# Graph attention beside experts: gathers issued at another pace, last softmax piece and lane carry ahead of the last expert unit

## The reference, cut to what matters

```python
# graph attention, 4 heads x 4 experts = 16 columns; 32768 random edges, and one self loop per node
h = (x @ W_gat).reshape(M, HEADS, NUM_EXPERTS)
e = leaky_relu(a_src[src] + a_dst[dst]); e_max = segment_max(e, dst); ee = exp(e - e_max[dst])
alpha = ee / (segment_sum(ee, dst)[dst] + 1e-16)
agg = segment_sum(h[src] * alpha[:, :, None], dst) + b_gat
scores = layernorm(agg).reshape(M, HEADS, NUM_EXPERTS).mean(1); top_k(scores, 2) -> softmax -> gates
# dense experts, all four on all rows
for ei in range(4):
    out += g_ei * (gelu(x @ W1[ei] + b1[ei], approximate=False) @ W2[ei] + b2[ei])
```

## Time and profile before

| | |
|---|---|
| median of 3 runs | 2281.04 us (2280.89 to 2281.67) |
| the profiled execution's own time | 2285.36 us |
| its span in the profile | 2283.6 us |
| busy: PE, DVE, POOL, ACT | 1666.2, 1276.7, 1076.5, 712.2 us |
| mean granted share of PE's clock | 0.851 |
| gathers of the stage (L1490), first and last start | 777.6 and 1153.7 us |
| up 19 on PE ends; the 37 steps end | 1131.3 us; 1236.0 us |

### The profile page before, as it was taken

How to read it: one execution, slowest core, us unless ns; L and a number is a source line. 1 busy time by engine, 2 the same in 40 slices (tenths; PEclk the granted TensorE clock), 3 DMA queues, 4 the chain that set the end, 5 groups by cost and what they waited for, 6 DMA issues and landing times. The chain is left out here.

```text
span 2283.6 us, 32653 instructions
## 1 busy us (share of the span) xinstructions
PE 1666.2 (73%) x8780; PEld 1319.3 (58%) x8781; DVE 1276.7 (56%) x3698; ACT 712.2 (31%) x1566; POOL 1076.5 (47%) x1102
## 2 busy tenths in 40 slices
PE   2776566766777799999934646565756799996997
PEld 1444344444445577777723546555645699984786
DVE  7877777667677410222146636555656566656235
ACT  1001146555651222222204632232323233312222
POOL 1676666555660566666640065555555554300000
PEclk9987578788789799999966867777777799997999
DMA  5233233333332122232251543433333565611001
GB/s 165 78 89 92 73 98 104 96 104 103 101 97 74 29 70 70 69 91 70 76 158 8 177 129 117 133 118 118 116 112 114 166 219 197 201 37 42 0 1 57
DMA packets 165026, 226.82 MB, mean 99 GB/s; under 512 B 35764, under 2 KB 124118, under 8 KB 162070
## 3 DMA queue, kind: packets, MB, share of 16 engines
q0 software_dynamic: 47392, 105.58, 16.5%
q1 hardware_dynamic: 114176, 115.99, 15.7%
q10 hardware_dynamic: 3318, 3.59, 0.5%
HBM read 172.48 MB, written 105.03 MB: 122 GB/s over the span
## 5 line engine op out<-in xcount | busy, mean ns | idle before, releaser
L473 POOL DMA_INDIRECT edge_rows<-xn_table,edge_source x391 | 376.5, 963 | 402.2 <-ACT held L2111 177.6
L2123 PE MATMUL part<-coef,held 128*128 128x128 f32 x2368 | 400.8, 317 | 215.7 <-issue 181.0
L473 POOL DMA_INDIRECT shared_space<-xn_table,edge_source x391 | 402.4, 1029 | 277.8 <-issue 108.5
L2123 PEld LDWEIGHTS part<-coef,held 128*128 128x128 f32 x2368 | 371.4, 228 | 254.6 <-issue 199.3
L2161 DVE SCALAR_TENSOR_TENSOR window_sums<-window_sums,fine_keep,part 128x256 f32 x592 | 282.4, 477 | 295.9 <-remote 130.2
L763 PE MATMUL part<-shared_space,hot 128*128 x832 | 297.9, 495 | 123.9 <-issue 63.4
L2111 ACT ACTIVATE held<-edge_rows 128x256 f32 x592 | 213.9, 408 | 484.6 <-PE part L2123 228.3
L1490 POOL DMA_INDIRECT gall<-attention_table,attention_source x256 | 244.9, 957 | 132.5 <-issue 68.3
L763 PEld LDWEIGHTS part<-shared_space,hot 128*128 128x128 f32 x832 | 176.7, 239 | 194.2 <-issue 173.4
L1148 DVE TENSOR_TENSOR shared_space<-shared_space,part 128x257 f32 x416 | 174.6, 420 | 132.8 <-remote 43.5
L2148 DVE SCALAR_TENSOR_TENSOR coef<-iota,fine_target,slot_coefs 128x128 f32<-128x128 f32 x592 | 203.7, 346 | 6.8 <-PEq L1283 6.8
(11 more groups left out here) (467 smaller groups left out, 1926.4 us busy)
## 6 DMA issues: line engine op xcount, KB each, us to landing
basis_sums<-window_sums SPq DMA_DIRECT2D x74, 1024.0 KB
z<-basis_sums SPq DMA_DIRECT2D x21, 1024.0 KB
expert_rows<-ys SPq DMA_DIRECT2D x20, 640.0 KB
shared_space<-expert_rows SPq DMA_DIRECT2D x25, 512.0 KB, 4.7
W<-in_L_ffn_W SPq DMA_DIRECT2D x20, 512.0 KB
gall<-attention_digits SPq DMA_DIRECT2D x32, 256.0 KB
xn_table<-shared_space SPq DMA_DIRECT2D x10, 640.0 KB, 4.1
shared_space<-xn_table,edge_source POOLq DMA_INDIRECT x391
```

Of the source, the lines that this page charges most:

```text
L473: pool.indirect_dma_start(rows[:, b % ring, 0:D], None, table, bass.IndirectOffsetOnAxis(ap=esrc[:, b:b + 1].bitcast(U32), axis=0)).then_i ...
L2123: mm = nc.tensor.matmul(part[n][:, c * P:(c + 1) * P], held[n][:, c * P:(c + 1) * P], coef[n][:, :, :].rearrange("p b w -> p (b w)"), star ...
```

## The change

Five things are edited together. (1) The gate ahead of group i of the gathers is at 9i/16 halves instead of 5i/8, so that a group is let go every 0.5625 halves instead of every 0.625, and the last at 35.4 halves instead of 39.4. (2) The pieces start behind units 6, 11, 15 and 17. (3) The last piece is no longer cut up between tiles: it runs as a whole behind unit 17, with its exponentials in the middle of ACT's unit 19, and the lane step ENDS follows at once. (4) On PE the four small blocks stand ahead of down 19 instead of behind it; on DVE the work along the lanes stands ahead of unit 19's tiles. For this the small blocks use PSUM banks 0 and 1 (of `up`), and the steps' banks move. (5) `ended` lies in the first weight buffer instead of in `hid`, so that POOL may gather the ends as soon as up 18 is through and the sums are stored; the blocks of the 37 steps move to the second weight buffer, and PE waits for the last tile's evacuation ahead of step 1.

```diff
-AFTER_UNIT = [8, 14, 18, 19]
+AFTER_UNIT = [6, 11, 15, 17]
 def experts_before(i):
-    half, part = divmod(5 * i, 8)
+    half, part = divmod(9 * i, 16)
...
-        return kind, done * per + per * part // 8
+        return kind, done * per + per * part // 16
...
+        ended = free[:, 0:NT * EW].rearrange("p (t w) -> p t w", w=EW)          # free is W1[0]
...
-        lines_ps = ps[0:GW, 7, :].rearrange("p (n q) -> p n q", n=4)
-        carry_ps = ps[:, 6, 0:EW]
+        lines_ps = ps[0:GW, 0, :].rearrange("p (n q) -> p n q", n=4)
+        carry_ps = ps[:, 1, 0:EW]
...
             pool.wait_ge(sums_out, 16 * PIECES)
+            pool.wait_ge(h_ready, (UNITS - 1) * 2 * FC)
...
-                for c in range(PIECES):
-                    if min(AFTER_UNIT[c] + 2, UNITS - 1) == m:
+                    if m == UNITS - 1 and n == FC - 1:
+                        exponents(PIECES - 1)
+                for c in range(PIECES - 1):
+                    if AFTER_UNIT[c] + 2 == m:
                         exponents(c)
...
-            down(UNITS - 1)
+            pe.wait_ge(h_used, UNITS * 2 * FC)
             pe.wait_ge(carry_steps, ENDS)
             nc.tensor.matmul(lines_ps[:, 0, :], sums[:, GT - 1, 0:GW], att.after[:, :], start=True, stop=True)
...
+            down(UNITS - 1)
             pe.wait_ge(carry_steps, RUN)
...
+            pe.wait_ge(y_used, UNITS * CT)
             turn_relations(0)
...
             for m in range(UNITS):
+                if m == UNITS - 1:
+                    carry_lanes()
...
                         parts = piece(c)
                         next(parts)
+                        if c == PIECES - 1:
+                            for _ in parts:
+                                pass
+                            lane_ends()
```

More of the change, by code:

```diff
@@ L1343, in attention_and_experts @@
         done = hid[0][:, :, :].rearrange("p f n -> p (f n)")
-        ended, crossed = (done[:, n * NT * EW:(n + 1) * NT * EW].rearrange("p (t w) -> p t w", w=EW) for n in range(2))
-        done = done[:, 2 * NT * EW:]
+        crossed = done[:, 0:NT * EW].rearrange("p (t w) -> p t w", w=EW)
+        done = done[:, NT * EW:]
         acc, sq = (done[:, n * NT * C16:(n + 1) * NT * C16].rearrange("p (t k) -> p t k", k=C16) for n in range(2))
@@ L1835, in piece, with lane_ends, carry_lanes @@
                 yield
+            by_head = lambda x: x[:, 0:C16].rearrange("p (h e) -> p h e", e=EXPERTS)
+            def lane_ends():
+                link.note(V.tensor_copy(by_head(last_top[:, :]), sums[:, GT - 1, GW:EW].unsqueeze(2).to_broadcast([P, H, EXPERTS])))
+                link(V.tensor_copy(last_top[:, C16:GW], sums[:, GT - 1, GW:EW]))
+                dve.sem_inc(carry_steps, 1)
+            def carry_lanes():
+                dve.wait_ge(carry_replies, LINES)
+                link.note(V.tensor_copy(first_of[:, :], lines_ps[:, 2, :]))
+                link(V.tensor_copy(chained[:, :], lines_ps[:, 3, :]))
+                link(V.tensor_tensor(chained[:, :], chained[:, :], first_of[:, :], ALU.mult))
+                link.note(V.tensor_scalar(chained[:, :], chained[:, :], BIG, -BIG, ALU.mult, ALU.add))
+                link(V.tensor_tensor(run[:, :], lines_ps[:, 1, :], first_of[:, :], ALU.mult))
+                link(V.tensor_scalar(first_of[:, :], first_of[:, :], BIG, -BIG, ALU.mult, ALU.add))
+                link(V.tensor_tensor(first_of[:, :], first_of[:, :], run[:, :], ALU.add))
+                link(V.tensor_tensor_scan(peak[:, 1:P + 1], chained[:, :], first_of[:, :], -BIG, ALU.add, ALU.max))
+                link.note(V.tensor_tensor(factor[:, 0, :], peak[:, 0:P], peak[:, 1:P + 1], ALU.subtract))
+                link(V.tensor_tensor(factor[:, 1, :], first_of[:, :], peak[:, 1:P + 1], ALU.subtract))
+                link(V.tensor_tensor(factor[:, 0, :], factor[:, 0, :], chained[:, :], ALU.add))
+                link(V.tensor_scalar(factor[:, :, :], factor[:, :, :], 0.0, None, ALU.min))
+                dve.sem_inc(carry_steps, 1)
+                dve.wait_ge(carry_replies, EXPONENTS)
+                link(V.tensor_tensor(first_of[:, :], factor[:, 1, :], lines_ps[:, 0, :], ALU.mult))
+                link(V.tensor_tensor_scan(run[:, :], factor[:, 0, :], first_of[:, :], 0.0, ALU.mult, ALU.add))
+                dve.sem_inc(carry_steps, 1)
             parts = iter(())
             for m in range(UNITS):
+                if m == UNITS - 1:
+                    carry_lanes()
                 for t in range(CT):
```

34 lines of the change are left out of this document (5 added, 29 removed).

## The result

The changed kernel takes **2294.87 us** (median of 16 runs, 2284.35 to 2304.71) against **2283.77 us** (16 runs, 2280.55 to 2289.53) of the kernel before, measured together: a ratio of 1.0048, 95% interval 1.003 to 1.0065. It is slower by 0.5%, 11 us. The forecast was 2276.0, with 2250 to 2290 as its range, so it had the sign wrong, and the range missed the time too.

What follows compares the result with a forecast made beforehand. It took PE to be bound by results arriving late while POOL issues gathers without pause. Experts 31 us longer and tail 36 us shorter gave -5 us, 2276.0 us against the median, range 2250 to 2290.

Steps and rivals of the forecast that it cites:

- 31: Experts: with the gate at 9/16 POOL sets the pace, and up 19 ends 31 us later, at 1162.
- -36 us: From up 19's end to the last step's: 69 us instead of 104.8, so 36 us shorter (33 to 38.5).
- the failed step: Tail: SP's loads of expert rows land about when the steps end; priced at nothing, up to 2 us if tight.
- such a case: Tail: POOL runs through all 26 gathers, first result 5 us later, steps end at 72; 66.3 if it pauses, 69 taken.
- I take 48: POOL's pauses before the last group's start: between 43 and 57 us, 48 taken, so that group starts at 1141.
- the third rival: Experts: POOL pauses as before, PE stands at the gate; up 19 at 1172 or later, time 2286 to 2292; chance 0.23.
- the case above: Main case, whole kernel: up 19 ends at 1162 (1154 to 1172), time 2270 to 2283 us; chance 0.45.
- The theory of late results: Experts and tail: while POOL issues gathers without pause, PE's results reach ACT and DVE late; 2.4 to 3 us pauses clear it.

Runs made afterwards that it cites:

- the second pair: Profiles of the kernel before and the changed kernel, both unchanged, taken again; they took 2282.95 us (ratio 1.000) and 2293.79 us (ratio 1.0039).

## Why the prediction was wrong

**Where the sum failed.** The terms were 31 and -36 us, together -5; measured were +35.3 and -28.1, together +7.2. So the cost was 4 us too small and the gain 8 us too large, and the larger miss, the failed step, is in the tail: SP's loads of expert rows beside the 37 steps, priced at "nothing", cost 6.1 us. Apart from these loads the mechanisms of both terms were right. With either term alone as measured and the other as predicted the sum would have been near zero (-0.7 or +2.9). The text said that an error of 1 part in 7 in either takes the difference away.

**The tail: 28 us instead of 36.** Up to the first step it is close: piece ready at 3.0 (predicted 3.5), ends' gathers at 5.9 (7.7), carry at 34.7 (35.7), first step at 38.0 (38.5). The term that was mis-sized is the 37 steps at 0.772 us from the first on, 27.8 us; they took 38.5. Some 4 to 5 us of it are results late beside POOL's last six gathers, also in the kernel with its loads held back; the prediction had 5 us for such a case and took the middle. The other 6.1 are what holding SP's loads back took away (38.5 and 32.4 us); the prediction said "nothing; up to 2 us" for them, and asked only when they land. Their landing cost nothing; they cost by what they kept from PE. That moving the loads takes the gaps away is shown. That it is PE's instructions which wait behind them is read from "issue", from a stop among products without a wait, and from the queues' rows, and wasn't measured by itself.

**The gate: the right mechanism, 4 us too small.** The prediction put the last group 9 us earlier than before ("I take 48" of pauses) and up 19's end 31 us later. Measured, POOL's stretch hardly changed: 374.2 and 374.9 us in the two profiles of the change, 376.1 and 374.4 in those of before, 371.7 with the gate alone. Its pauses come to the same sum at both gates, and why is not shown. The last group is let go at 35.4 halves instead of 39.4. If it is let go at the same moment, and PE stands as near to the gate, PE is 4 halves later everywhere behind it, 4 x 8.61 = 34.4 us. Found were 35.3 us in the change, 34.4 in the second pair and 33.1 with the gate alone (386.8 - 353.7). The closeness is in part luck. Before, up 19's end lay 18.6 us ahead of the last group's start, where 1.375 halves make 11.8; now it lies 18.6 us behind it, where 2.56 halves make 22.0. And the profile with the loads held back has 395.4 us with the same gate, 6 us above the changed kernel's 389.0 and 389.7. It is nearly the third rival's mechanism, "POOL pauses as often as before, and PE stands exactly at the gate", which had up 19 at 1172 or later; I gave it 0.23. On before's clock up 19 ended at 777.6 + 389.0 = 1166.6, inside the 1154 to 1172 of the case above and just short of the 1167 behind which the prediction called itself wrong.

The extra time is of two kinds, which the sum had not kept apart. Windows of the experts, of before and of the change:

```profile
785.00:1131.00 346.00, 329.51 (x1336) 255.72 (x1337) 60.72 (x166) 87.35 (x161) 226.39 (x237) 0.98 0.26 75
```

```profile
793.00:1174.50 381.50, 343.09 (x1332) 260.82 (x1332) 75.58 (x218) 91.47 (x166) 240.66 (x251) 0.95 0.26 70
```

PE is idle 38.4 us instead of 16.5. The same products take 13.6 us more, and the granted clock is a mixture of 2.4 and 1.2 GHz more often (0.95 instead of 0.98). That second part stood only as a remark in the third rival.

**The theory of late results** held where it was tried at the level of before's profile: they go with half the gathers, follow the gathers into the steps, and the gate alone makes the loss. Its blind spot was that nothing in the one profile tells that it depends on the level: at 2014 us the same gathers are issued at the same 1.25 us, and nothing is late.

**The range.** Its upper end left out most of the third rival (2286 to 2292), which it should have held. Of the 11 us measured, the stage has 7.2 in the first pair of profiles and 11.8 in the second; the rest of the first pair lies outside the stage and isn't the change's work as far as is shown.

## What to carry to other kernels

When two engines pace each other through a gate, don't ask only what a looser gate lets one of them do earlier; look for the stretch that stays (here POOL's, 372 to 376 us at both gates of the upper level), and count by how many steps the other is then behind when the last is let go. A load moved beside a stretch of very short instructions isn't free because its data is wanted late: here it cost 6 us of 38, by the reading above because PE ran out of instructions. A piece of work that waits for gathers is placed by when the last of them lands: behind unit 17 DVE stood 16.66 us for them, behind unit 18 0.28 us. And where two large terms cancel, price each small one that lies beside them; 8 us in one of them decided the sign here.

## What the runs showed of the hardware

- The same program ran at about 2014 us in four groups of runs and at 2260 to 2284 us in two (three with the first measurement), once on the same chip. With the gate at 9/16, up 19 ended 317.0 us behind the first gather at 2014 us, where PE was never idle, and 386.8 us at 2260 us. What sets the level is open.
- At the upper level products of PE reached an idle DVE up to 20.6 us late while POOL issued indirect DMAs back to back: with the ends' gathers held back, PE ended a step's products at 1210.53, and DVE, free, took them at 1231.15. Pauses of POOL of 2.5 to 3.6 us let them through.
- PE stopped for 3.19 us in the middle of 12 products without a wait, while loads held the DMA engines at 94.8%; before, with the queues free there, the same steps ran at 0.772 us each, and with the loads held back no such stop was left.
